# A depthwise convolution's taps moved from VectorE to ScalarE and GpSimd, in a four-layer kernel

## The reference

```python
x = x + layer0(gn(x))   # 3x3 depthwise conv, SSD block, 3x3 depthwise conv, layer norm + MLP
x = x + layer1(gn(x))   # projection to 384, 3x3 depthwise conv + SiLU, selective scan in 4 directions, gate, projection
x = x + layer2(gn(x))   # 3x3 depthwise conv
x = x + layer3(gn(x))   # 3x3 depthwise conv
```

```python
out[y, x] = bias + sum(w[dy + 1, dx + 1] * src[y + dy, x + dx] for dy in (-1, 0, 1) for dx in (-1, 0, 1))
```

## Time and profile before

| | |
|---|---|
| median of three executions | 30251.23 us (30236.49 to 30252.84) |
| the profiled execution | 30252.72 us, its span 30251.1 us |
| TensorE busy | 25716.8 us, 85% |
| VectorE busy | 25150.6 us, 83% |
| ScalarE busy | 19750.8 us, 65% |
| GpSimd busy | 20979.6 us, 69% |
| mean granted TensorE clock | 0.93 |

### The profile page before, as it was taken

One profiled execution on the slowest core, in us unless ns is written; L12 is line 12 of the kernel. 1 busy time (PEld: TensorE's weight loads), 2 busy tenths in 40 slices (PEclk: granted clock), 3 DMA queues, 4 the chain that ended last, 5 costly groups with the idle time before them and its releaser, 6 DMA issues. The chain is left out here.

```text
span 30251.1 us, 298846 instructions
## 1 busy us (share of the span) xinstructions
PE 25716.8 (85%) x78624; PEld 11949.9 (40%) x78624; DVE 25150.6 (83%) x28280; ACT 19750.8 (65%) x36872; POOL 20979.6 (69%) x9230
## 2 busy tenths in 40 slices
PE   8888888888888887888878888888888888888888
PEld 4344333443334433344333443334433344333443
DVE  6899867998679986799867998689986899868998
ACT  4677646776467764678646776467764677646776
POOL 2689726897268972699726897268972689726897
PEclk8999989999899998999989999899998999989999
DMA  0111101111011110111101111011110111101111
GB/s 8 49 58 59 46 9 48 58 59 46 9 48 58 59 46 9 48 58 58 46 10 48 58 59 46 9 48 58 59 47 8 49 58 59 46 8 49 59 59 46
DMA packets 844582, 1330.53 MB, mean 44 GB/s; under 512 B 226176, under 2 KB 243456, under 8 KB 839680
## 3 DMA queue, kind: packets, MB, share of 16 engines
q1 hardware_dynamic: 842752, 1309.85, 14.3%
HBM read 1241.87 MB, written 67.63 MB: 43 GB/s over the span
## 5 line engine op out<-in xcount | busy, mean ns | idle before, releaser
L1588 PE MATMUL ps<-arena,ident 128*128 128x512 f32 x24576 | 12192.6, 616 | 0.0
L1809 DVE TENSOR_TENSOR_SCAN arena<-ps,arena 128x512 f32<-128x512 f32 x6912 | 8605.5, 1266 | 275.8 <-ACT ps L1669 272.0
L1492 POOL TENSOR_TENSOR arena<-arena 128x1536 f32<-128x1536 f32 x2320 | 8003.7, 3450 | 577.5 <-DVE arena L1809 572.8
L1809 DVE TENSOR_TENSOR_SCAN arena<-arena,ps 128x512 f32<-128x512 f32 x5376 | 6668.7, 1266 | 116.4 <-ACT arena L1669 71.5
L1588 PEld LDWEIGHTS ps<-arena,ident 128*128 128x128 f32 x24576 | 4420.4, 198 | 3843.7 <-issue 3636.5
L1669 ACT ACTIVATE ps<-arena 128x512 f32<-128x512 f32 x6912 | 4748.1, 687 | 1571.9 <-DVE arena L1809 1551.0
L1753 POOL TENSOR_TENSOR arena<-arena 128x1536 f32<-128x1536 f32 x1536 | 5309.5, 3457 | 599.5 <-ACT arena L1640 599.3
L1606 PE MATMUL ps<-ident,scaled 128*128 128x128 f32 x21504 | 3432.6, 287 | 1567.0 <-DVE arena L1809 1278.4
L1786 DVE TENSOR_TENSOR arena<-arena,ps 128x512 f32<-128x512 f32 x6144 | 4073.3, 663 | 811.3 <-issue 666.6
L1606 PEld LDWEIGHTS ps<-ident,scaled 128*128 128x128 f32 x21504 | 2691.9, 147 | 4687.8 <-DVE arena L1809 2944.5
L1653 ACT ACTIVATE scaled<-arena,cols 128x384 f32<-128x384 f32 x7168 | 3969.8, 601 | 253.1 <-PE ps L1606 250.1
(11 more groups left out here) (181 smaller groups left out, 31426.0 us busy)
## 6 DMA issues: line engine op xcount, KB each, us to landing
arena<-rows SPq DMA_DIRECT2D x3904, 256.0 KB, 3.3
spare<-rows SPq DMA_DIRECT2D x520, 256.0 KB, 3.4
arena<-x SPq DMA_DIRECT2D x16, 1536.0 KB, 13.2
x<-arena SPq DMA_DIRECT2D x16, 1536.0 KB, 10.7
arena<-x SPq DMA_DIRECT2D x64, 384.0 KB, 8.5
out<-arena SPq DMA_DIRECT2D x64, 384.0 KB, 3.0
rows<-xd SPq DMA_DIRECT2D x264, 64.0 KB, 1.6
arena<-L_conv_fc_w SPq DMA_DIRECT2D x16, 576.0 KB, 5.4
```

The lines of the kernel that those rows point to most:

```text
L1492: return nc.gpsimd.tensor_tensor(three(dbu[:, no % DB, :]), du[:, par, :, :], each, ALU.mult)
L1588: nc.tensor.matmul(m.ps[:, t, :], m.ident[:, :], x, start=False, stop=(no == order.last_sum(b, t))).then_inc(at["y_mm"], 1)
L1809: nc.vector.tensor_tensor_scan(flip(hs[:, g % HS, here]), flip(decays), flip(adds), carry[:, k, N2 * n + t:N2 * n + t + 1], ALU.mult, ALU. ...
```

## The change

Some taps leave VectorE (and TensorE). They are called "beside": tap 7 (the row below, same column), and in some convolutions tap 1 (the row above) too. Neither shifts columns, so for them a strip's source is one contiguous stretch. ScalarE multiplies the source by the tap's weight into a side buffer (`products`, a Copy activation with the weight as scale). There are four side buffers of two strips each (`AHEAD`, `side`), in two free slots. GpSimd adds the second product, where there are two, into the first, then the residual, where there is one (`gather`, one step ahead), and, once the strip is evicted, adds the side buffer to it (`side_added`). Where tap 7 falls outside the plane the last row of the side buffer is cleared first. ScalarE refills a side buffer when its step's last add is done. In the convolution with SiLU the eviction is now an Identity, and a separate Silu follows GpSimd's add, two steps later (`through_silu`).

Three settings replace the rule for TensorE's taps:

- TWO, the first two convolutions: taps 7 and 1 beside, TensorE three taps (4, 3, 5) in each step from 1 on, VectorE 7 in step 0 and 4 in the others.
- WIDE, the 384 channels: the same over 12 steps.
- ONE, layers 2 and 3: tap 7 beside, TensorE 3, 3, 4, 4, 3, 3, 4 taps, VectorE 8 in step 0, then 5, 5, 4, 4, 5, 5, 4.

```diff
+AHEAD = 4
+TWO, ONE, WIDE = dict(beside=(7, 1), pe_share=(0, 3, 3, 3, 3, 3, 3, 3)), dict(beside=(7,), pe_share=(0, 3, 3, 4, 4, 3, 3, 4)), dict(beside=(7, 1), pe_share=(0, 3, 3, 3, 3, 3, 3, 3, 3, 3, 3, 3))
...
+        self.side = m.slots(side, 2, parts).rearrange("p a (b c l) -> p (a b) c l", b=2, c=2) if side is not None else None
...
     def pe_taps(i):
-        return () if i == 0 else PE_TAPS[:3] if i <= 2 else PE_TAPS
+        return PE_TAPS[:pe_share[i]]
 
     def dve_taps(i):
-        own = [tap for tap in range(9) if tap not in pe_taps(i)]
+        own = [tap for tap in range(9) if tap not in pe_taps(i) and tap not in beside]
         return own if i else [CENTRE] + [tap for tap in own if tap != CENTRE]
...
-        if residual is not None:
-            @block.gpsimd
-            def _(pool):
+        @block.gpsimd
+        def _(pool):
+            gathers = max(own - 1, 0) + (residual is not None)
+
+            def gather(i):
+
+                n, (t, r) = gathers * i, steps[i]
+                whole_side = side[:, i % AHEAD, 0, :]
+                for j, tap in enumerate(beside):
+                    t, ya, height, _ = moved(i, tap)
+                    pool.wait_ge(side_done, own * i + j + 1)
+                    if j == 0 and height < ROWS:
+                        nc.gpsimd.memset(whole_side[:, height * W:], 0.0).then_inc(filled, 1)
+                        pool.wait_ge(filled, t + 1)
+                    if j:
+                        part = whole_side[:, (ya - r) * W:(ya - r + height) * W]
+                        nc.gpsimd.tensor_tensor(part, part, side[:, i % AHEAD, j, 0:height * W], ALU.add).then_inc(gathered, 1)
+                if residual is not None:
...
+                    nc.gpsimd.tensor_tensor(whole_side, whole_side, rows(residual, t, r), ALU.add).then_inc(gathered, 1)
+
+            if own:
+                gather(0)
+                for i, (t, r) in enumerate(steps):
+                    if i < last:
+                        gather(i + 1)
+                    pool.wait_ge(taken, i + 1)
+                    if gathers:
+                        pool.wait_ge(gathered, gathers * (i + 1))
+                    nc.gpsimd.tensor_tensor(rows(dst, t, r), rows(dst, t, r), side[:, i % AHEAD, 0, :], ALU.add).then_inc(side_added, 1)
...
         @block.scalar
         def _(act):
+            def products(i):
+                if i >= AHEAD and own:
+                    act.wait_ge(side_added, i - AHEAD + 1)
+                for j, tap in enumerate(beside):
+                    t, _, height, sa = moved(i, tap)
+                    nc.scalar.activation(side[:, i % AHEAD, j, 0:height * W], src[:, t, sa * W:(sa + height) * W], ACT.Copy,
+                                         scale=w[:, t, tap:tap + 1]).then_inc(side_done, 1)
+
+            def through_silu(i):
+                t, r = steps[i]
+                act.wait_ge(side_added, i + 1)
+                nc.scalar.activation(rows(dst, t, r), rows(dst, t, r), ACT.Silu).then_inc(silu_out, 1)
+
+            for i in range(AHEAD):
+                products(i)
             for i, (t, r) in enumerate(steps):
                 act.wait_ge(tapped, tapped_all[i])
                 nc.scalar.activation(rows(dst, t, r).rearrange("p (a b) -> p a b", a=2), banks(i),
-                                     ACT.Silu if silu else ACT.Identity, bias=bcol[:, t:t + 1]).then_inc(taken, 1)
+                                     ACT.Silu if silu and not own else ACT.Identity, bias=bcol[:, t:t + 1]).then_inc(taken, 1)
+                if silu and own and i >= 2:
+                    through_silu(i - 2)
+                if i and i - 1 + AHEAD <= last:
+                    products(i - 1 + AHEAD)
+            if silu and own:
+                through_silu(last - 1)
+                through_silu(last)
...
-            conv3x3(m, s23, s45, taps, loads=loads)
+            conv3x3(m, s23, s45, taps, loads=loads, **TWO)
...
-            conv3x3(m, xa, xc, taps, silu=True, loads=loads)
+            conv3x3(m, xa, xc, taps, silu=True, loads=loads, **WIDE)
...
-            conv3x3(m, s23, s45, taps, residual=s01)
+            conv3x3(m, s23, s45, taps, residual=s01, **ONE)
```

More of the change, by code:

```diff
@@ L235, with __init__ @@
     NAMES = ("taps_loaded", "centre")
-    def __init__(self, m, n, parts, weight, bias, own=False, slot=SLOTS):
+    def __init__(self, m, n, parts, weight, bias, own=False, slot=SLOTS, side=None):
         self.m, self.n, self.parts, self.weight, self.bias, self.own = m, n, parts, weight, bias, own
@@ L260, in gpsimd, with conv3x3 @@
                                         w[:, t, tap:tap + 1], None, ALU.mult)
-def conv3x3(m, src, dst, taps, residual=None, silu=False, out=None, loads=()):
+def conv3x3(m, src, dst, taps, residual=None, silu=False, out=None, loads=(), beside=(), pe_share=()):
     nc, n, parts = m.nc, taps.n, taps.parts
@@ L269, in conv3x3 @@
     last = len(steps) - 1
+    side = taps.side
     def pe_taps(i):
-        return () if i == 0 else PE_TAPS[:3] if i <= 2 else PE_TAPS
+        return PE_TAPS[:pe_share[i]]
     def dve_taps(i):
-        own = [tap for tap in range(9) if tap not in pe_taps(i)]
+        own = [tap for tap in range(9) if tap not in pe_taps(i) and tap not in beside]
         return own if i else [CENTRE] + [tap for tap in own if tap != CENTRE]
@@ L288, in rows, with moved @@
         return v[:, t, r * W:(r + ROWS) * W]
+    def moved(i, tap):
+        t, r = steps[i]
+        (ya, yb, _, _), (sa, _, _, _) = window(tap, r, r + ROWS)
+        return t, ya, yb - ya, sa
     def banks(i):
         return m.ps[0:parts, (2 * i) % 8:(2 * i) % 8 + 2, :]
-    with Stage(nc, "taps_mm", "taken", "tapped", "whole", "stored", "brought") as (taps_mm, taken, tapped, whole, stored,
-                                                                                    brought), nc.Block() as block:
+    own = len(beside)
+    with Stage(nc, "taps_mm", "taken", "tapped", "side_done", "filled", "gathered", "side_added", "silu_out", "stored", "brought") as (
+            taps_mm, taken, tapped, side_done, filled, gathered, side_added, silu_out, stored, brought), nc.Block() as block:
         @block.sync
@@ L2025, in layers @@
             weights, loads = scan_weights(m, l1)
-            conv3x3(m, xa, xc, taps, silu=True, loads=loads)
+            conv3x3(m, xa, xc, taps, silu=True, loads=loads, **WIDE)
             selective_scan(m, xc, y, weights, rows)
             finish_scan(m, y, s01, x1v, l1)
-            taps = Taps(m, NH, P, l2["w"], l2["b"])
+            taps = Taps(m, NH, P, l2["w"], l2["b"], side=10)
             group_norm(m, s01, s23, taps, have_stats=True)
-            conv3x3(m, s23, s45, taps, residual=s01)
-            taps = Taps(m, NH, P, l3["w"], l3["b"])
+            conv3x3(m, s23, s45, taps, residual=s01, **ONE)
+            taps = Taps(m, NH, P, l3["w"], l3["b"], side=10)
             group_norm(m, s45, s23, taps)
-            conv3x3(m, s23, s01, taps, residual=s45, out=ob)
+            conv3x3(m, s23, s01, taps, residual=s45, out=ob, **ONE)
             nc.all_engine_barrier()
```

16 lines of the change are left out of this document (10 added, 6 removed).

## The result

The changed kernel takes 30007.19 us, the median of four runs (30000.86 to 30015.56), against 30252.03 us (30236.49 to 30269.31). The ratio is 0.9916, with a 95% interval of 0.9904 to 0.9927: 245 us, 0.8%, faster. The forecast was 29945 us, 307 us faster, in a range of 29870 to 30050. The sign and the range held; a fifth of the gain is missing. In a later comparison on one chip the changed kernel took 30002.08 us (29998.12 to 30009.13), ratio 0.9905 [0.9888, 0.9921].

A forecast was written before the change was run, and what follows sets the result against it. VectorE's taps were taken to bound five barrier-enclosed convolution stages; savings of 9.7, 7.0, 4.4, 3.8 and 15.4 us, 40.3 a sample, less the walk's shortfall gave 38.3, 307 us for eight samples: 29945 us, range 29870 to 30050.

The forecast's parts named there:

- The walk through the convolutions: Five convolution stages, each engine's queue followed in order from the stage's start: 38.3 us a sample saved.
- The sum: Whole kernel: 38.3 us a sample saved in the convolutions, 307 us for eight samples, giving 29945 us.
- That VectorE's taps bound the stages, and that their saving shows in the stages one to one: All five convolutions: VectorE's taps are on the path, 2354.0 us busy; stages shrink to 51, 48.5, 57, 57 and 70 us.
- TensorE as the new pacemaker, by little: Middle of the convolutions: TensorE needs 10.14 us a pair of steps, VectorE 9.5, so VectorE waits about 1 us a pair.
- GpSimd at 2.34 us an add, not blocked by the taps: Convolutions: two adds a step take 4.7 us, hidden behind TensorE's 5.07, with VectorE's taps not slowing them.
- the rival of blocked adds: Convolutions: each GpSimd add waits out a tap, 3.53 us; 222 us worse in all, 30475 us; chance 5%.
- The tail of four adds: End of a convolution: add 5, gather 7, add 6 and add 7 in one GpSimd queue, 4 x 2.34 = 9.4 us.
- A product of 1.11 us, between 1.05 and 1.26: Convolutions: time of one ScalarE multiplication of a strip by a tap's weight, hidden behind TensorE even at 1.26 us.
- What a stage saves, the span saves: Five convolution stages, each shut in by barriers: every microsecond saved there was taken to shorten the whole execution equally.
- Rival 2: Convolutions: queueing, slower products or a lower clock for longer; 2.6 us adds cost 7.7 us a sample, 30007 us; chance 12%.

The follow-up runs named there:

- the first trace: The changed kernel's first profiled execution, from the comparison with the kernel before that measured 30007.19 us against 30252.03 us.
- the second of before: The kernel before, unedited, run and traced once more: 30268.26 us.
- a version that wins 73 us in its own stages: Changed kernel with gathers two steps ahead and no taps beside in the last step of the first three convolutions: 29994.82 us, ratio 0.9908 to the kernel before.

## Why the prediction was right, and where it wasn't

The walk through the convolutions was right in mechanism and size. The sum took all other stages as unchanged, and they weren't; the range had room for that, but for other reasons.

- **That VectorE's taps bound the stages, and that their saving shows in the stages one to one**: right. The five forecasts of 51, 48.5, 70, 57 and 57 us met 51.6, 48.6, 70.2, 57.0 and 56.8.
- **TensorE as the new pacemaker, by little**: right. It works without a gap through the first three stages, and VectorE waits 0.7 to 1.0 us a pair; relieving it brought 1.7 to 3.5 us a stage.
- **GpSimd at 2.34 us an add, not blocked by the taps**: right. Its adds took 2.352 us at the median and 2.407 at most, though next to taps and products alike, so the rival of blocked adds fell. The read port that the Trainium skill names in "Perfetto Trace Analysis", section Optimizing Scalar/DVE Operations, doesn't show for this form of tap (one operand in SBUF, one in PSUM).
- **The tail of four adds**: right, 3.3 us behind the last eviction; two gathers ahead took off 0.8 to 1.0 us in four of the stages and 0.4 in the last.
- **A product of 1.11 us, between 1.05 and 1.26**: it took 1.135 at the median as an instruction, and eight took 8.32 us in a row, 1.04 each. Hidden, as said.
- **The sum**: 8 x 38.3 is 306, not 307, which changes nothing.
- **"What a stage saves, the span saves"**: this is the step that failed. The barriers keep the work of one stage out of the next, but not the granted clock: by where a stage starts among its changes, unchanged code takes 464 or 471 us. The sum had no term for it: the SSD stage took 6.9 us a sample more in the first trace and 3.0 in the second against the second of before, 55 and 24 us. Rival 2 named a granted clock that is lower for longer, but with no stage and no price for it. Its price of 30007 us for other things is the measured median, by chance: it came from adds of 2.6 us, and the adds took 2.352. The scan stage, 2681.6 to 2690.6 us a sample over the traces, moves the total by up to 72 us between the extremes, of the size of what was to be told apart.

## What to carry to other kernels

In a stage between barriers, walk each queue with rates from starts, the order at the end included: that gave five stages to 0.6 us, and showed which reordering would pay. Then look at the unchanged stages too, trace against trace, before explaining a shortfall in the changed ones; where TensorE's clock goes up and down, their lengths move by more than many a gain, and a version that wins 73 us in its own stages may show 12. A gain of under 0.2% in such a kernel should be read from the stages it touches, and confirmed by more than one execution.

## What the runs showed of the hardware that was not expected

- The SSD stage, of unchanged code, falls on steps from sample to sample: of 112 stages 20 take 464.2 to 464.6 us and 39 take 471.1 to 472.0, the others lie between 460.8 and 480.7. Its length goes with the time at which TensorE's clock is granted at 1.2 GHz, from 121 to 175 us.
- Two such stages of one trace run alike to 0.15 us for 32 us; then the clock is granted at 0.50 in one and 1.00 in the other, and twelve matmuls take 8.58 against 5.39 us. Their first rise of the clock had come 25.87 and 25.63 us after the start.
- Idle matmuls up to the end of the stage ahead didn't change what was granted 40 us later, 0.74.
- With ScalarE's products added beside them, GpSimd's adds, VectorE's taps and TensorE's passes keep the rates of before: 2.35, 1.19 and 0.43 us.
